# A macaron block (feed-forward, pooled attention, feed-forward) on one core: the order within a pipeline step set anew on three engines

## Time and profile before

| | |
|---|---|
| median of 3 runs | 165.23 us |
| the profiled execution | 165.78 us |
| its span, first to last instruction | 164.0 us |
| TensorE (matmul) busy | 154.6 us, 94% |
| VectorE busy | 134.8 us, 82% |
| ScalarE busy | 124.9 us, 76% |
| GpSimd busy | 109.5 us, 67% |
| the chain that ended last | TensorE 43%, VectorE 27%, GpSimd 20% of the span |

### The profile page before, as it was taken

The page is one execution under the profiler, slowest core; times in us unless marked ns, Lnnn a source line. Parts: engine busy times, 40 slices in busy tenths (PEclk is TensorE's granted clock), DMA queues, the critical chain, the costliest instruction groups (busy, mean ns, idle before and its releaser), DMA issues.

```text
span 164.0 us, 2561 instructions
## 1 busy us (share of the span) xinstructions
PE 154.6 (94%) x767; PEld 102.6 (63%) x767; DVE 134.8 (82%) x384; ACT 124.9 (76%) x233; POOL 109.5 (67%) x165
## 2 busy tenths in 40 slices
PE   6999999999999999999999999899999999999931
PEld 6784746576757758476576675565666757465411
DVE  1685389888899999999999898999999999745541
ACT  3257798999995968859899586776885868898960
POOL 1229208999899686997999979979959485350200
PEclk9999999999999999999999999999999999999995
DMA  4990000000000000000000020000020202020222
GB/s 134 251 284 18 0 6 0 0 0 0 2 6 0 0 2 0 0 4 0 0 0 0 4 64 2 0 0 2 4 64 0 64 0 64 6 64 0 64 64 66
DMA packets 10286, 5.08 MB, mean 31 GB/s; under 512 B 1056, under 2 KB 10144, under 8 KB 10272
## 3 DMA queue, kind: packets, MB, share of 16 engines
q1 hardware_dynamic: 9744, 4.66, 9.7%
q10 hardware_dynamic: 528, 0.26, 0.5%
HBM read 2.82 MB, written 2.10 MB: 30 GB/s over the span
## 4 chain that ended last, share of the span: by engine, by line
PE 43%; DVE 27%; POOL 20%; issue 4%; DMA 3%; ACT 1%; ACTq 0%; DVEq 0%; POOLq 0%
PE work L659 19%; DVE inv_sum L509 8%; POOL normed L301 5%; PE hidden L621 5%; PE hidden L625 4%; PE hidden L622 4%; POOL rstd L293 4%; POOL normed_att L301 4%; DVE pooled L513 3%; POOL share L323 3%; PE work L633 3%; PE hidden L678 3%; DMA fc_raw<-in_L_ffn_W_fc_dram 3%; POOL rstd_att L293 2%; DVE weight_sum L501 2%
## 5 line engine op out<-in xcount | busy, mean ns | idle before, releaser
L659 PE MATMUL work<-square,proj_t 128*128 128x512 f32 x128 | 63.2, 599 | 0.4 <-DVE square L477 0.4
L366 ACT ACTIVATE signs<-work 128x512 bf16<-128x512 f32 x80 | 44.6, 605 | 15.2 <-PE work L659 15.2
L352 ACT ACTIVATE relu<-hidden 128x512 f32<-128x512 f32 x64 | 38.8, 605 | 8.0 <-PE hidden L625 7.9
L293 POOL TENSOR_TENSOR rstd<-var_eps,minus_half 128x4 f32<-128x4 f32 x16 | 21.0, 1311 | 21.6 <-DVE neg_mean L441 21.6
L659 PEld LDWEIGHTS work<-square,proj_t 128*128 128x128 f32 x128 | 21.9, 189 | 15.4 <-ACT square L357 6.9
L357 ACT ACTIVATE square<-relu 128x512 f32<-128x512 f32 x46 | 29.3, 636 | 0.8
L621 PE MATMUL hidden<-in_hi,fc_lo 128*128 128x512 f32 x64 | 27.8, 434 | 0.0
L509 DVE RECIPROCAL inv_sum<-weight_sum 128x256 f32<-128x256 f32 x16 | 27.6, 1735 | 0.0
L625 PE MATMUL hidden<-in_lo,fc_hi 128*128 128x512 f32 x64 | 25.4, 397 | 0.0
L622 PE MATMUL hidden<-in_hi,fc_hi 128*128 128x512 f32 x64 | 25.1, 392 | 0.0
L323 POOL TENSOR_TENSOR share<-weight,inv_sum 128x256 f32<-128x256 f32 x16 | 12.7, 795 | 6.5 <-DVE inv_sum L509 6.5
(11 more groups left out here) (85 smaller groups left out, 253.7 us busy)
## 6 DMA issues: line engine op xcount, KB each, us to landing
x_first<-_attn_hidden_states_dram SPq DMA_DIRECT2D x8, 256.0 KB, 4.2
out_dram<-x_out SPq DMA_DIRECT2D x8, 256.0 KB, 2.2
fc_raw<-in_L_ffn_W_fc_dram ACTq DMA_DIRECT2D x1, 256.0 KB, 4.2
proj_raw<-in_L_ffn_W_proj_dram SPq DMA_DIRECT2D x1, 256.0 KB, 4.4
att_raw<-in_L_attn_Wk_dram SPq DMA_DIRECT2D x1, 64.0 KB, 4.0
att_raw<-in_L_attn_Wv_dram SPq DMA_DIRECT2D x1, 64.0 KB, 3.6
att_raw<-in_L_attn_Wka_dram SPq DMA_DIRECT2D x1, 64.0 KB, 3.7
vectors<-in_L_attn_bk_dram SPq DMA_DIRECT2D x1, 0.5 KB, 3.2
```

The source lines that it names most:

```text
L293: nc.gpsimd.tensor_tensor(rstd[kind][:], var_eps[kind][:], minus_half[:], ALU.pow).then_inc(rstd_made[kind], 1)
L352: nc.scalar.activation(relu[j.lane][:, c, :], hidden[c][:], ACT.Relu).then_inc(relu_made[j.lane], 1)
L366: nc.scalar.activation(signs[j.lane][:, k, :], work[j.lane][:], ACT.Sign, bias=bias, scale=scale).then_inc(signs_made[j.lane], 1)
L659: mm = nc.tensor.matmul(work[j.lane][:], proj_t[:, c, :], square[j.lane][:, c, :], start=(c == CONTRACT_ORDER[0]), stop=(c == CONTRACT_ORD ...
```

## The change

No instruction is added or removed. On three engines the order within a step is another. (`ff_dve_square` now takes the chunk rather than its place in a list; both calls now stand at the end of VectorE's step, where the one that did anything stood already.)

ScalarE:

```diff
                 for j in feed_forward(i - 1):
                     ff_sign(j, 2)
-                    ff_sign(j, 3)
+                for b in attention(i):
+                    att_weight(b)
                 for j in feed_forward(i):
                     ff_relu(j, 1)
                 for j in feed_forward(i - 1):
+                    ff_sign(j, 3)
+                for j in feed_forward(i):
+                    ff_square(j, 1)
+                for b in attention(i):
+                    att_key(b)
+                for j in feed_forward(i):
+                    ff_relu(j, 2)
+                for j in feed_forward(i - 1):
                     ff_sign(j, 4)
-                for b in attention(i):
-                    att_weight(b)
-                for j in feed_forward(i):
-                    ff_square(j, 1)
-                    ff_relu(j, 2)
+                for j in feed_forward(i):
                     ff_square(j, 2)
                     ff_relu(j, 3)
-                for b in attention(i):
-                    att_key(b)
-                for j in feed_forward(i):
                     ff_square(j, 3)
```

VectorE:

```diff
                 for j in feed_forward(i - 2):
                     ff_sum_sign(j, 1)
+                    ff_sum_sign(j, 2)
                 for b in attention(i - 2):
                     att_invert(b, 0)
+                for b in attention(i - 1):
+                    att_sum(b)
                 for b in attention(i - 3):
                     att_add(b)
-                for j in feed_forward(i - 2):
-                    ff_sum_sign(j, 2)
-                for j in feed_forward(i - 1):
-                    ff_dve_square(j, 1)
                 for b in attention(i - 2):
                     att_invert(b, 1)
-                for j in feed_forward(i - 2):
-                    ff_sum_sign(j, 3)
-                    ff_sum_sign(j, 4)
...
-                for b in attention(i - 1):
-                    att_sum(b)
+                for j in feed_forward(i - 2):
+                    ff_sum_sign(j, 3)
+                    ff_sum_sign(j, 4)
                 for j in feed_forward(i):
                     if j.index > 0:
                         ff_lo(j)
+                for b in attention(i):
+                    att_part_lo(b)
                 for b in attention(i - 2):
                     att_pool(b)
-                    att_product(b)
                 for j in feed_forward(i - 2):
                     ff_add(j)
-                for b in attention(i):
-                    att_part_lo(b)
+                for b in attention(i - 2):
+                    att_product(b)
                 for b in attention(i + 1):
                     att_layer_norm(b)
                 for j in feed_forward(i):
                     ff_dve_square(j, 0)
+                    ff_dve_square(j, 1)
```

```diff
-                for b in attention(i - 3):
-                    att_turn_back(b)
-                for j in feed_forward(i - 1):
-                    ff_expand(j, 2)
-                for b in attention(i - 1):
-                    att_key_attention(b)
-                for j in feed_forward(i - 1):
-                    ff_expand(j, 3)
-                    ff_contract(j, 0)
-                for b in attention(i - 1):
-                    att_keys(b)
                 for j in feed_forward(i):
                     ff_turn(j)
                 for j in feed_forward(i - 1):
-                    ff_contract(j, 1)
                     ff_contract(j, 2)
                 for b in attention(i):
                     att_turn(b)
-                for b in attention(i - 2):
-                    att_values(b)
                 for j in feed_forward(i - 1):
                     ff_contract(j, 3)
                 for j in feed_forward(i - 2):
                     ff_count(j)
+                for b in attention(i - 2):
+                    att_values(b)
...
                 for j in feed_forward(i):
                     ff_expand(j, 0)
+                for b in attention(i):
+                    att_key_attention(b)
+                for j in feed_forward(i):
                     ff_expand(j, 1)
...
+                for j in feed_forward(i):
+                    ff_expand(j, 2)
+                for b in attention(i):
+                    att_keys(b)
+                for b in attention(i - 2):
+                    att_turn_back(b)
+                for j in feed_forward(i):
+                    ff_expand(j, 3)
+                    ff_contract(j, 0)
+                    ff_contract(j, 1)
```

More of the change, by code:

```diff
@@ L407, in _ @@
                 for j in feed_forward(i - 1):
-                    ff_sign(j, 4)
-                for b in attention(i):
-                    att_weight(b)
+                    ff_sign(j, 3)
                 for j in feed_forward(i):
                     ff_square(j, 1)
-                    ff_relu(j, 2)
-                    ff_square(j, 2)
-                    ff_relu(j, 3)
                 for b in attention(i):
@@ L418, in _ @@
                 for j in feed_forward(i):
+                    ff_relu(j, 2)
+                for j in feed_forward(i - 1):
+                    ff_sign(j, 4)
+                for j in feed_forward(i):
+                    ff_square(j, 2)
+                    ff_relu(j, 3)
                     ff_square(j, 3)
@@ L470, in att_part_lo, with ff_dve_square @@
                                         ALU.subtract).then_inc(lo_made["att"], 1)
-            def ff_dve_square(j, n):
-                if n < len(j.dve_squares):
-                    c = j.dve_squares[n]
+            def ff_dve_square(j, c):
+                if c in j.dve_squares:
                     wait_relu(dve, j, c)
```

## The result

The changed kernel takes 160.46 us (four runs, 160.41 to 161.06) against 165.35 of the kernel before beside it (165.22 to 165.69): ratio 0.9709, with a 95% interval of 0.9681 to 0.9738 (in brackets from here on). The direction was right; the size fell outside the range of 161.0 to 165.0. The profiled executions are 160.51 against 165.78 us, so 0.4 of their 5.3 us comes from the profiled run of before lying above its median.

The account below looks back on a forecast made before the run. TensorE bounds it to 41.8 us, VectorE with GpSimd to 117.5, then TensorE. Terms -1.05 - 0.6 - 0.75 - 0.4 - 0.4 = -3.2, plus 0.4, give -2.8: 162.4 us against the median, range 161.0 to 165.0.

Parts of the forecast that it names:

- Start, -1.05: TensorE's first steps: contraction 1 before the next turning fills a wait, 0.86 us, plus about 0.2 in step 1; -1.05.
- Low part before the residual, -0.6: VectorE near 41.80 us: low part ahead of the residual, so its closed run of work begins 0.6 us sooner.
- the cover that I named: VectorE's wait for the count, 0.38 us plus 0.42 before the job's low part, was to hide the 0.6 us.
- VectorE from 44.4 to 118.6: VectorE's middle: same work, time lost in waits and slowed scans falls from 2.2 to 1.4 us; -0.75, bounds -2.2 and +0.5.
- In full steps VectorE is the bound: Steps with all eleven VectorE pieces: 11.5 us on VectorE against 10.7 on TensorE.
- Where TensorE takes over, -0.4: Steps 11 and 12: less work left behind the turning back, 0.9 us better, less some 0.4 waiting for a product.
- +0.4 for scans in the middle of a normalising: Full steps: `att_pool` scans that find GpSimd normalising lose 0.1 us each in four steps; 0.4 us against the gain.
- Steps 14 and 15, -0.4: Last steps, where ScalarE sets the period by relu and square of one chunk in a row: about 0.2 each.
- ScalarE as the bound: Rival, chance 0.22: third square comes late in steps 6, 12, 13 and 15, middle saves nothing; small gain, 164.3 us.
- GpSimd as the chain: Rival, chance 0.12: if normalising ends over 0.8 us later, each of six sums costs 0.95; slower, 168.4 us.
- VectorE gives it back: Rival, chance 0.06: VectorE starts sooner, but chunk 3 waiting for `ff_add` makes each full step as late; 165.2 us.
- The signs: Trace marks of a right forecast: first reciprocal about 42.8, no `pooled` wait, 1.7 us shares, product of attention 9 near 116.

Follow-up runs that it names:

- the short reciprocal: The kernel before, lightened on VectorE: second half of each reciprocal cut from 256 to 128 columns; 164.56 us, 0.994.
- the low part early: The kernel before with one VectorE edit: the attention's low part moved from behind `ff_add` to right behind that of the job; 165.18 us, 0.9987.
- both together: The kernel before with the second reciprocal half cut to 128 columns and the attention's low part moved ahead; 163.02 us, 0.986.

## Why the prediction missed, step by step

- **Start, -1.05: right, with a little luck.** Job 5 begins its expansions 1.07 earlier, of which 0.15 is the earlier contraction 0; and contraction 1 alone gave 0.7. Contraction 1 follows contraction 0 without a gap (four matmuls from 12.58).
- **Low part before the residual, -0.6: too large.** The first reciprocal is 1.50 earlier, of which 1.07 is the start: 0.43 is left. With this edit alone it moved from 44.41 to 44.18: the low part began at 41.45 and the residual only at 42.06, past the 41.80 at which it began in the kernel before. The reason is in the cover that I named. Of its two waits only the 0.38 us lies behind the job's low part, where the attention's now stands, and 0.6 us of work don't fit in it.
- **VectorE from 44.4 to 118.6: the step that failed.** "Term: -0.75; bounds -2.2 and +0.5"; measured -2.89 (74.16 to 71.27), outside both bounds. I had kept 1.4 us of the lost time by assuming that the sum and one scan would start late behind GpSimd in five steps. None did: the sums take 1174 ns on average instead of 1373, and it is GpSimd's attention normalising that pays, 601 ns a piece instead of 478. And I held the sum of prices, 71.95, for a floor, though one of them contained a wait: a scan and the product that reads it were 1.26 apart and are 1.13 from scan to residual now, the sum 1.07 instead of 1.13. By distances of starts, the six sums of the stretch take 6.52 us instead of 7.84, the six `att_pool` scans 6.80 instead of 7.54, and the wait of 0.78 is gone: 2.84 of the 2.89 us. The two experiments on these places give the term from the other side: put back alone, the sum's place makes the stretch 2.07 us longer, the product's 1.28. (The stretch is seven steps, 5 to 11, not eight, and the prices were added up for seven.)
- **"In full steps VectorE is the bound": half of it.** The kernel before had a second bound beside it, the ring with GpSimd, which the short reciprocal, the low part early and both together show. My replay had that ring's two shortcuts in it (the low part out, no share blocked by the late sum) but paid nothing for them, since VectorE at 11.5 a step hid them.
- **Where TensorE takes over, -0.4, and +0.4 for scans in the middle of a normalising: neither is there.** The shift of VectorE's step 12 (4.39) and of TensorE's job 12 (4.54) differ by 0.15. TensorE never waits from 42 to 117, though VectorE's full step of 11.28 is longer than its 10.76. The full step is one of seven: TensorE needs 71.61 us from the turning of job 5 to that of job 12 (46.36 to 117.97), and VectorE's seven steps take 71.27. So the lag of the full step is taken from slack of the lighter ones, and the middle ends before it is used up. How near it comes: the low part of step 11's attention is ready at 111.89, its key attention begins at 112.35.
- **Steps 14 and 15, -0.4: about right in size, but not in place.** The table has 0.46 from job 12 to the last contraction (4.54 to 5.00). Job 14 begins its expansions 4.74 earlier (138.29 instead of 143.03), so steps 14 and 15 gave 0.26 of it and steps 12 and 13 the other 0.20.
- **The rivals.** ScalarE as the bound: the idle time before its relus grew, from 5.0 to 8.8 us in the middle, but its third square came in time and TensorE's light period stayed 8.95 (8.94 before). GpSimd as the chain: 1% of the chain. Its condition was met, but not its consequence: the normalising ended some 2 us later than forecast, and the second share no longer waited for its reciprocal (it began at 98.40, the reciprocal having ended near 98.0). But the normalising had paid for the sum, the shares kept their 0.73, and 0.58 us were left before the scan. VectorE gives it back: no.
- **The signs.** Met: the first reciprocal at 42.91 (42.8 forecast), no wait of `pooled` for `share_key` in the middle. Failed: "shares of about 1.7 us beside every sum". The replay had the share begin as the first reciprocal ends, 1.76 us into the step; in step 10 it begins 3.9 us into it (96.91), behind a normalising that the forecast took to be over by then. The product of attention 9 began at 113.52, not near 116, as the failed term says.

Sum by the trace: 1.07 + 0.43 + 2.89 + 0.15 + 0.71 = 5.25, the last being from job 12 to the last residual; 0.15 of the first and 0.25 of the last are chance.

The Trainium skill ("SBUF — State Buffer", the reading of its port diagram) was weighed against the sum's new place. The Trainium skill also says there that of the two instructions the one that starts first keeps the port pair, and the other blocks. The traces mostly agree: in the lightened kernel before, a share that began just behind a sum took 1.65 us, and in the kernel after the normalising, four instructions, took 2.66 instead of 1.75; the last section has the exceptions. What the prediction got wrong is therefore not the rule but the moment: behind the first reciprocal the sum starts when GpSimd is mostly in a normalising of four short pieces, and not in a share that VectorE itself waits for. That it is the moment and not the neighbouring instruction is read from the timelines; no run here moved a GpSimd instruction by itself, so it stays argued.

## What to carry to other kernels

An engine that is busy for 96% of a stretch need not be its only bound: follow every ring that crosses to another engine and back, and price it beside the sum of each engine, because relieving one bound alone shows nearly nothing (1.0 and 0.2 us) and both together show the gain (2.4). A price taken as a distance of starts holds any wait between the two instructions, so a sum of such prices is no floor. And orders written out by hand on several engines are one object: each of the three, undone alone, cost more than twice what all three had won.

## What the runs showed of the hardware, unexpectedly

- A scan and the VectorE instruction that reads it are 1.26 us apart, a scan and one that doesn't read it 1.13 (100.52 to 101.65). In these rows an independent instruction between them is worth 0.13 us.
- Which instruction pays where a scan meets GpSimd mostly follows from the order of their starts. The sum at 49.02 began just after a share and took 1.68 us. That at 94.67 began inside a normalising of four pieces and took 1.16, and the normalising took 2.66 instead of 1.75.
- Two kinds of exception stand in the traces. In the kernel before, a scan that began at 51.27, 0.08 us after GpSimd's `rstd` (128x4, L293, at 51.19), was not held up: 1.23 and 1.01 us, both as alone. And in the lightened kernel before, a share product began at 48.08, 0.02 us ahead of the sum, and still was the one that paid, 1.77 us instead of 0.73.
